# A two-layer graph attention kernel: row sums on ScalarE, and a paced gather

## The reference, cut to what matters

```python
h = jnp.maximum(_layernorm(x, axis=-1), 0.0)
x = x + _L0_gnn_ref(h, adj, ...)      # attention over 16 heads, @ W_out + b_out, elu
h = jnp.maximum(_layernorm(x, axis=-1), 0.0)
x = x + _L1_gnn_ref(h, adj, ...)

def _L1_gnn_ref(...):
    q = sent_embed @ W_q.T + b_q
    k = sent_embed @ W_k.T + b_k
    v = sent_embed @ W_v.T + b_v
    z = scale * (q @ k.T)
    spare_z = z * adj_tensor
    spare_z = jnp.where(spare_z == 0.0, -10000.0, spare_z)
    attn = jax.nn.softmax(spare_z, axis=1)
    return jax.nn.relu(attn @ v)
```

## Time and profile before

| what | value |
|---|---|
| median of 3 runs | 454.66 us (454.53 to 454.87) |
| the profiled execution | 451.98 us, of which the span from the first to the last instruction is 450.1 us |
| mean granted TensorE clock | 0.954 of full speed |
| busy in the span | PE 393.3 us, DVE 368.4, POOL 255.9, ACT 245.7 |

### The profile page before, as it was taken

One profiled execution on the slowest core, in us unless ns is written; L12 is line 12 of the kernel. 1 busy time (PEld: TensorE's weight loads), 2 busy tenths in 40 slices (PEclk: granted clock), 3 DMA queues, 4 the chain that ended last, 5 costly groups with the idle time before them and its releaser, 6 DMA issues.

```text
span 450.1 us, 6244 instructions
## 1 busy us (share of the span) xinstructions
PE 393.3 (87%) x2058; PEld 281.5 (63%) x2070; DVE 368.4 (82%) x731; ACT 245.7 (55%) x511; POOL 255.9 (57%) x268
## 2 busy tenths in 40 slices
PE   7999999998799998999977997978998999968860
PEld 4888887786588886886554755645656855434430
DVE  3999999986899999998799999689854568989900
ACT  4379777783999999872442443343433346142220
POOL 2335151321868866876786535883524777788640
PEclk9599999999899999999996999989999999989995
DMA  8988999710000023435755432763212676679941
GB/s 322 395 347 316 380 313 350 272 50 25 4 6 6 7 29 91 103 112 151 232 155 148 151 95 87 208 208 112 95 47 96 193 207 200 200 171 130 127 61 19
DMA packets 26996, 70.02 MB, mean 156 GB/s; under 512 B 7892, under 2 KB 8148, under 8 KB 24788
## 3 DMA queue, kind: packets, MB, share of 16 engines
q0 software_dynamic: 13056, 38.45, 32.4%
q1 hardware_dynamic: 13904, 31.16, 19.0%
q10 hardware_dynamic: 4, 0.00, 0.0%
HBM read 52.47 MB, written 17.13 MB: 155 GB/s over the span
## 4 chain that ended last, share of the span: by engine, by line
POOL 28%; DVE 16%; issue 15%; PE 11%; DMA 2%; ACT 1%; DVEq 0%; POOLq 0%
PE psum L1349 7%; POOL s_shared L1271 7%; POOL s_shared L1300 5%; POOL out_dram L1284 4%; POOL s_shared L1252 3%; POOL s_rs L1282 3%; DVE s_shared L814 3%; DVE s_shared L812 3%; DVE s_shared L1044 3%; POOL s_x L1290 2%; POOL s_early L1300 2%; PE psum L1450 2%; DVE s_x L828 2%; DVE s_shared L821 1%; DVE h_t L1044 1%
## 5 line engine op out<-in xcount | busy, mean ns | idle before, releaser
L1101 ACT ACTIVATE s_shared<-psum,seq_all 128x320 bf16<-128x320 f32 x192 | 81.9, 571 | 6.0 <-PE psum L1349 4.3
L1349 PE MATMUL psum<-s_shared 128*128 128x198 bf16 x768 | 75.1, 254 | 9.6 <-POOL s_shared L1252 9.6
L1349 PEld LDWEIGHTS psum<-s_shared 128*128 128x128 bf16 x768 | 67.9, 98 | 17.4 <-POOL s_shared L1252 9.9
L563 PE MATMUL psum<-w_seq,hT 128*128 128x272 f32 x256 | 63.3, 402 | 0.4 <-ACT w_seq L424 0.4
L1371 PE MATMUL psum<-w_out,hT 128*128 128x512 f32 x128 | 61.4, 625 | 0.4
L563 PEld LDWEIGHTS psum<-w_seq,hT 128*128 128x128 f32 x256 | 49.0, 195 | 10.2 <-ACT w_seq L424 0.5
L1393 PE MATMUL psum<-w_qk,s_early 128*128 128x257 f32 x240 | 54.5, 379 | 0.0
L1393 PEld LDWEIGHTS psum<-w_qk,s_early 128*128 128x128 f32 x240 | 44.3, 189 | 6.0
L1271 POOL DMA_INDIRECT s_shared<-seq_dram,tab x30 | 37.4, 1246 | 11.3 <-issue 8.9
L1371 PEld LDWEIGHTS psum<-w_out,hT 128*128 128x128 f32 x128 | 26.2, 205 | 26.3 <-issue 25.4
L282 POOL TENSOR_TENSOR rstd<-veps,power 128x1 f32<-128x1 f32 x16 | 8.9, 558 | 54.9 <-DVE veps L468 54.9
(11 more groups left out here) (267 smaller groups left out, 742.1 us busy)
## 6 DMA issues: line engine op xcount, KB each, us to landing
adj_ring<-in_adj_dram SPq DMA_DIRECT2D x16, 1024.0 KB, 7.8
seq_dram<-seq_all POOLq DMA_DIRECT2D x16, 264.0 KB, 4.0
x_ring<-in_x_dram SPq DMA_DIRECT2D x16, 256.0 KB, 8.2
h_dram<-h_t SPq DMA_DIRECT2D x16, 256.0 KB, 2.3
w_seq<-in_L_gnn_W_seq_dram SPq DMA_DIRECT2D x1, 1024.0 KB, 5.5
w_q<-in_L_gnn_W_q_dram SPq DMA_DIRECT2D x1, 1024.0 KB, 13.5
w_k<-in_L_gnn_W_k_dram SPq DMA_DIRECT2D x1, 1024.0 KB, 15.7
w_v<-in_L_gnn_W_v_dram SPq DMA_DIRECT2D x1, 1024.0 KB, 8.6
```

Of the source, the lines that this page charges most:

```text
L563: last = pe.matmul(bank[2 + 2 * (t % 2) + i][:, 0:SX // 2], hT[:, t % 2, c * P:(c + 1) * P], w_seq[:, c, i * (SX // 2):(i + 1) * (SX // 2) ...
L1101: last = act.activation(ind[i][:, j, PAD:], bank[4 + i][:, 0:LN], ACT.Sign, bias=seq_all[:, j, D + n:D + n + 1])
L1349: last = pe.matmul(acc(i)[:, k, 0:3 * W2], ind[i][:, j, k * P:(k + 1) * P], rhs.rearrange("p t w -> p (t w)"), start=(j == 0 and k != 1), ...
```

## The change

There are two parts.

First layer: VectorE's `accumulate` goes. `copy_h1T` becomes four copies of 128 x 128, each of which also writes its row sums into a column of `col`; one reduction over the 16 columns and four matmuls with the identity give the sum of all rows. The tile without neighbours is now transposed and copied too, since its sum is needed. TensorE's `queries(EARLY)` moves ahead of the matmuls of the sum. On VectorE `norm_bias` moves: behind `scores` at k of 4, 6 and 8, and between the product and the additions of `aggregate` at k of 12 and 13. ScalarE's and POOL's waits on the accumulation go.

Second layer: the gather of row k waits for dot k - 6, or for the last dot ahead of its own tile where that comes sooner.

```diff
@@ -51,6 +51,7 @@
 H1T_FREE = {2: 2, 3: 2, 4: 3, 5: 3, 6: 4, 7: 4, 8: 6, 9: 8}
+HEAVY = [k for k in range(T) if SLOTS[SEQ[k]] > 1]
 GROUPS = [(6, 8, 10), (5,), (7,), (9,), (11,), (12, 14), (13, 15)]
@@ -711,7 +712,8 @@
         assert at <= SHARED
-        h_acc = spare[2]
+        col = spare[2][:, 0:C * T].rearrange("p (c t) -> p c t", c=C)
+        col_sum = spare[2][:, C * T:C * T + C]
         e = [bout_bc[:, :], u_bias_bc[:, 0:D]]
@@ -738,7 +740,7 @@
         def h1_no(t):
-            return t + (t < NO_SLOT)
+            return t + 1
 
@@ -750,7 +752,7 @@
         x_late = [sem(f"x_late{t}") for t in range(T - X_EARLY)]
-        x1_stored, h_sum_mm = sem("x1_stored"), sem("h_sum_mm")
+        x1_stored, h_sum_mm, weighed = sem("x1_stored"), sem("h_sum_mm"), sem("weighed")
 
@@ -772,6 +774,7 @@
 
+        LEAD = 6
         ROWS_EARLY = FLAT_ROWS + C + LONE + 1
@@ -874,7 +877,7 @@
 
-                def aggregate(k):
+                def aggregate(k, tile=None):
                     t = SEQ[k]
@@ -891,7 +894,10 @@
                     w = sc[:, o:o + K, :].unsqueeze(3).to_broadcast([P, K, H, DH])
-                    step(dve.tensor_tensor(rows, rows, w, ALU.mult))
+                    dve.tensor_tensor(rows, rows, w, ALU.mult).then_inc(weighed, 1)
+                    if tile is not None:
+                        norm_bias(tile)
+                    dve.wait_ge(weighed, HEAVY.index(k) + 1)
                     last = dve.tensor_tensor(hb, G(t)[:, 0, 0:D], G(t)[:, 1, 0:D], ALU.add)
@@ -922,14 +928,6 @@
 
-                def accumulate(t):
-                    dve.wait_ge(h1_done, t + 1)
-                    if t == 0:
-                        dve.tensor_copy(h_acc[:, :], h_t[:, 0, :]).then_inc(summed, 1)
-                    else:
-                        dve.wait_ge(summed, t)
-                        dve.tensor_tensor(h_acc[:, :], h_acc[:, :], h_t[:, t % 2, :], ALU.add).then_inc(summed, 1)
-
                 def lone_totals(b):
@@ -969,25 +967,26 @@
                 aggregate(3)
-                for k in range(1, T + 2):
-                    if k - 1 < T:
-                        residual(k - 1)
-                    if 0 <= k - 2 < T:
-                        accumulate(k - 2)
+                for k in range(1, T + 1):
+                    residual(k - 1)
                     if k - 1 in SCORES_AT:
...
                         lone_totals(k - 1)
-                    if k - 1 < T:
+                    behind = k >= 2 and k + 2 in HEAVY and k not in SCORES_AT and k - 1 not in SCORES_AT
+                    if k in SCORES_AT and k - 1 not in SCORES_AT and k > 2:
+                        scores(SCORES_AT[k])
+                        norm_bias(k - 1)
+                    elif not behind:
                         norm_bias(k - 1)
...
                         lone_rows(1)
-                    if k in SCORES_AT:
+                    if k in SCORES_AT and (k - 1 in SCORES_AT or k == 2):
                         scores(SCORES_AT[k])
                     if k >= 2 and k + 2 < T:
-                        aggregate(k + 2)
+                        aggregate(k + 2, k - 1 if behind else None)
                     if k == 6:
@@ -1049,6 +1048,8 @@
                 step(dve.memset(z[:, :, :], 0.0))
+                dve.wait_ge(h1T_done, T)
+                dve.tensor_reduce(col_sum, col, AX_X, ALU.add).then_inc(summed, 1)
                 constants(0, EARLY)
@@ -1126,7 +1127,10 @@
                         act.wait_ge(u_done, t - EARLY + 1)
-                    act.activation(h1T(t), bank[1], ACT.Copy).then_inc(h1T_done, 1)
+                    for c in range(C):
+                        last = act.activation(h1T(t)[:, c * P:(c + 1) * P], bank[1][:, c * P:(c + 1) * P], ACT.Copy,
+                                              accum_out=col[:, c, t:t + 1])
+                    last.then_inc(h1T_done, 1)
 
@@ -1138,7 +1142,7 @@
                         copy_u(U_AT[k])
-                    if k >= 2 and k - 2 != NO_SLOT:
+                    if k >= 2:
                         copy_h1T(k - 2)
@@ -1147,7 +1151,6 @@
                             act.wait_ge(h1_tr, h1_no(t - 2))
-                            act.wait_ge(summed, t - 1)
                             act.wait_ge(h1_stored[t % 2], 16 * (t // 2))
@@ -1293,6 +1296,8 @@
                         k = ROW1[t] + s
+                        if min(k - LEAD, ROW1[t]) > 0:
+                            pool.wait_ge(dot_done, min(k - LEAD, ROW1[t]))
                         if k == ROWS_EARLY:
@@ -1301,7 +1306,6 @@
                 pool.wait_ge(hid_ready, T - 2)
-                pool.wait_ge(summed, T)
                 pool.wait_ge(proj_done, T)
@@ -1415,10 +1419,13 @@
                 transposes_h1(T - 1)
-                pe.wait_ge(summed, T)
+                queries(EARLY)
+                pe.wait_ge(summed, 1)
                 pe.wait_ge(hidT_done, T)
-                pe.matmul(bank[0], ones[:, 0:P], h_acc).then_inc(h_sum_mm, 1)
-                for t in range(EARLY, T - 1):
+                for c in range(C):
+                    last = pe.matmul(bank[0][:, c * P:(c + 1) * P], col_sum[:, c:c + 1].to_broadcast([P, P]), ident[:, :])
+                last.then_inc(h_sum_mm, 1)
+                for t in range(EARLY + 1, T - 1):
                     queries(t)
@@ -1429,7 +1436,7 @@
                     if k == 1:
-                        pe.wait_ge(h1T_done, T - 1)
+                        pe.wait_ge(h1T_done, T)
                     for c in range(C):
...
                     last.then_inc(a_tr, 1)
```

## The result

The changed kernel takes 459.89 us (median of 4 runs, 458.68 to 460.48), the kernel before on the same chip 454.60: a ratio of 1.0116, 95% interval [1.0092, 1.0139], so 4.2 to 6.3 us slower. Forecast were 457.8 us and 453.8 to 461.8, slower with a chance of 0.71.

What follows compares the result with a forecast made beforehand. VectorE, with POOL behind it, was taken to bound the first layer; POOL's gathers, the last landing and dot 33 the second. Pacing's 10.4 us less the first layer's 7.3 gave 454.66 + 3.1 = 457.8 us, range 453.8 to 461.8.

Steps and rivals of the forecast that it cites:

- The first layer's 7.3 us: First layer: shorter VectorE work and moved norm_bias bring the first gather 7.3 us earlier, 339.7 in place of 347.00.
- none of that work goes: Between POOL's roots for tiles 7 and 8, its 9.18 us of store, gathers and loads stay; tiles 8 to 11 add 0.4.
- The 1.4 + 0.8 us for the product ahead of norm_bias: First layer, k of 12 and 13: product ahead of norm_bias gives 1.4 and 0.8 us, the second cut by TensorE.
- The 0.36 from 0.95 to 0.59: First layer: without the addition beside it POOL's root takes 0.59 not 0.95, so norm_bias comes 0.36 us earlier where uncovered.
- the last two tiles' 0.7: End of the first layer: the two last tiles give 0.36 us each, 0.7 of the sum.
- the sum's cover of 1 us: Start of the second layer: the later sum is ready about 349.5, the first dot at 350.49, leaving 1 us of cover.
- The pacing's 10.4 us: Second layer: gathers waiting for dots at rows 21 and 34 cost, seen alone, 3.1 + 7.3 = 10.4 us.
- Whatever happens to dot 33 happens to the end: From VectorE's last big tile to the end: dot 33 and POOL's stores come late by the same 3.1 us.
- (a): The forecast itself: +3.1 us, with 1.3 to 6.5 by landing time and a first-layer gain down to 4; chance 0.60.
- (b): Gathers land in 2.6 to 3.2 us, or the first layer gives 9: parts cancel, 454.2 to 455.6 us; chance 0.17.
- (c): The second layer's wait has no price, first-layer gain stays: 447.4 us; faster if dot 15 ends by 371.5; chance 0.12.
- (d): First layer gives 3 us or less, ScalarE's longer copies or TensorE standing in the way: 462 us or more; chance 0.11.

Runs made afterwards that it cites:

- e2: The kernel before with only the pacing of the gathers added, at a lead of 6: 463.84 us, ratio 1.0228 to the kernel before.
- e13: Changed kernel without pacing, norm_bias never behind the product, TensorE's list brought to the kernel before's length: 446.65 us, ratio 0.9865 to the kernel before.
- e8: The kernel before with 12 more warm-up matmuls on TensorE where it only waits: 456.43 us, ratio 1.0063 to the kernel before.
- e1: The changed kernel without the pacing wait of the gathers: 448.93 us, ratio 0.9913 to the kernel before.
- e11: Changed kernel without pacing, 4 warm-up matmuls in place of 8 ahead of layer 1, norm_bias never behind the product: 449.41 us, ratio 0.9924.

## Why the prediction came out right

**What bounds.** Right: POOL's gathers, the last landing and dot 33 decide; the chain after has them in the same order.

**The first layer's 7.3 us** were 7.18 at the first gather, but two of its terms were wrong and cancelled. Residual starts earlier by 4.0 us at tile 8 (285.90 before, 281.91 after; forecast 4.0), then by 6.4 at tile 11 where 4.4 was forecast, and by 6.4 still at tile 13 where 6.6 was. (1) The step "none of that work goes" failed. No instruction goes, but POOL's stretch between the roots of tiles 7 and 8 shrank from 9.18 to 8.15 us (277.81 to 285.96). The root gives 0.30 of that, and two issues, of a gather and of a load of x, give 0.67. Before and after:

```profile
287.02 1.12 POOL L1271 DMA_INDIRECT s_shared<-seq_dram,tab  x1 [0.30 <-issue]
288.45 1.45 POOL L1290 DMA_INDIRECT s_x<-in_x_dram,tab  x1 [0.30 <-issue]
```

```profile
282.46 0.95 POOL L1274 DMA_INDIRECT s_shared<-seq_dram,tab  x1 [0.30 <-issue]
283.72 0.95 POOL L1293 DMA_INDIRECT s_x<-in_x_dram,tab  x1 [0.30 <-issue]
```

Beside the 1.45 us ran the addition that is gone now (288.38 to 289.07). The next stretch gave 0.50 in the same way (9.43 and 8.93). Tiles 8 to 11 gave 2.4 us instead of 0.4. That the issues go by what VectorE does meanwhile is argued from such pairs of rows. (2) The 1.4 + 0.8 us for the product ahead of norm_bias were nothing. The forecast had TensorE cut the second of them; its timeline shows that it cut both, since it has no pause from 305.98 to 327 us, and the root's 1.47 and 2.00 us beside the product took VectorE's gain besides. The 0.36 from 0.95 to 0.59 and the last two tiles' 0.7 (0.78 measured: 7.18 - 6.40) held. That the sum of 7.3 came out as 7.18 is therefore luck: 2.0 us too little in one term and 2.2 too much in another.

**Additions.** ScalarE's copies cost 1.1 us a tile and hid; the sum's cover of 1 us held with 0.82 us to spare.

**The pacing's 10.4 us** held: row 21's gather at 375.45 (375.9 forecast), row 34 at 394.56 (394.5), row 39 at 401.18 (401.1). The path had one step that the forecast lacks: row 30 waited 0.89 us for dot 24, and with it for a third landing, row 26's 4.62 us. One term was small: the last landing took 4.91 and not 4.38, so dot 33 came at 406.11 and not at 405.4. By e2's ratio the whole is 10.3.

**From dot 33 to the end** the prediction moved everything by the same 3.1 us. That is the step that failed. Whatever happens to dot 33 happens to the end, the prediction said; but on the way TensorE's third gap grew to 6.51 us and its product ran at 1.2 GHz (1.1 to 1.3 us), and behind the last store the last branch of a list that got 21 instructions longer costs 3.4 us more. The forecast of 3.1 and the measured 5.3 (4.2 to 6.3) differ by 2.2. The runs add up by ratio: first layer with the cheap branch -1.35% (e13), branch +0.63% (e8), pacing with its loss of clock +2.05% (after against e1), in all +1.3%; measured +1.16%. So in the time the first layer is worth 6.1 us (5.1 to 7.1), less than the 7.3 of the forecast and less than the 7.18 at the first gather of the profiled executions; why is open.

The direction and the pacing's mechanism came out as forecast. That the time lies inside the range is in part luck: no term of the range stands for the branch or the clock, and together they are about 4 us. Two slips in the sums changed nothing: a fifth more than 4.38 is 5.26 and not 5.1, which makes the upper bound +4.9; and a first layer of 9 us gives +1.4 and does not cancel the pacing.

**The rivals.** (a) happened in its mechanism; 0.6 us of the miss is its size at dot 33 (3.73 for 3.1), the rest came behind it. (b) is out: landings were 4.4 to 4.9 us. (c) is out: dot 15 started at 374.49, not before 371.5; a lead of 12 is what (c) looks like. (d) is out: the first layer gave what it should.

## What to carry over

A wait that paces gathers by finished dots must leave room for issue, landing and dot together: here a lead of 12 cost nothing, and from 8 down to 6 each row cost about 2 us. Before an instruction is moved into another's waiting time, ask whether the two can run side by side at all, and whether another engine has slack left to pass the gain on. Here the moved product held up the very root that it was to cover, and TensorE was full behind it. And compare the stretch behind the last store as well: a few instructions more or less on the longest engine moved this kernel's end by 2.7 to 3.7 us, where the whole change made 5.3, so a change that adds instructions needs a control that adds as many and does nothing.

## What the hardware showed that was not expected

- TensorE's last branch takes 0.40 us or 3.1 to 4.1, by the length of its list, and not simply the shorter the better; twelve matmuls that do nothing made the kernel 2.9 us (1.7 to 4.0) slower.
- The issue of an indirect DMA on POOL takes longer beside some work of VectorE: the store of a tile took 1.02 us with VectorE idle (e11, 323.19) and 2.58 beside a product of 1536 columns (e11, 315.01), a gather 0.95 to 1.99 (before, 276.04).
- POOL's root of 128 values takes 0.58 us, 0.95 beside a 128 x 512 addition, 1.47 beside a product of 1024 columns and 2.00 beside one of 1536.
- A gather that has waited idle for a dot takes 1.16 us to issue, at all five places above; most others take 0.95.
